# Identity products ahead of TensorE's first work, and the last layer's weights folded between the first transposes

## The chip, the cores and the metric

The kernel runs on one core of a Trainium2 chip. The metric is device microseconds of one execution of the whole program; lower is better. The kernel is compared by the median of three executions. Engines are named as in the profile: PE is TensorE's matmul side and PEld its weight loads, DVE is VectorE, ACT ScalarE, POOL GpSimd, and SP the queue that issues most of the transfers. TensorE runs at one of two clocks, 1.2 and 2.4 GHz; a granted clock of 0.5 in a view is the lower, 1.0 the higher.

## What is computed

Four graph layers with a residual around each are applied to `x` (8 batches, 1024 nodes, 256 features) with the same dense weighted adjacency `adj` (8 x 1024 x 1024, mostly zeros). All data are float32.

```
h = relu(layernorm(x)); q, k = split(h @ Wqk); v = h @ Wv          # layer 0
agg = adj @ k; w = sum(q * agg) / 16;  x = x + softmax(w)[:, None] * v
h = relu(layernorm(x)); x = x + attention(h, 8 heads, scores * 2 adj) @ Wo + bo   # layer 1
h = relu(layernorm(x)); x = x + hypergraph(h, W1, b1, gamma, beta, W2, b2) + h    # layer 2
h = relu(layernorm(x)); Q = h Wq^T + bq; K = h Wk^T + bk; V = h Wv^T + bv         # layer 3
w = adj * exp(Q K^T); x = x + (w / rowsum(w)) @ V
```

Several products of weights alone are made once, before the loop over the batches, and used in all of them. Layer 0: Wq0 Wk0^T, so that `w` is the row sum of (h Wq0 Wk0^T) times (adj h). Layer 3: M3 = Wq3^T Wk3 in the same way, the vectors Wq3^T bk3 and Wk3^T bq3, and the number bq3 . bk3. Layer 2: gamma W2 and beta W2; layer 1: bv1 Wo1, which joins the output's bias.

## The kernel before, in words

The five engines run programs of their own, written out by hand in `build_program`, and meet by semaphores; no scheduler moves anything. The order of instructions in the code is the order in which each engine takes them, and an engine whose next instruction waits holds all that stand behind it. Batch 0 is written out for TensorE (`batch(0, True)`), the others run in a loop. Nodes stand in eight tiles of 128 (NT = 8), features in two of 128 (DT = 2). PSUM is `ps` with eight banks of 512 columns. An fp32 product shows as two MATMUL records, a transpose as one.

What matters here is the setup and the first stage of batch 0, about the first 40 us:

- SP issues the transfers in this order: `xn` (the batch's x, 1 MB), `mask`, `wqk0s` and `W0`'s right half (layer 0's weights, signalled by `weights0_in`), then fourteen under `weights_in`: seven vectors (L423), `w2s`, `Wo1`, the two halves of `w3s` (Wq3 and Wk3), and three broadcasts `bo1B`, `b2B`, `bv3B`. Behind them come `adjT` (4 MB), three weights `W1`, and `adjN` (4 MB). At last SP waits for `m3_made` and stores M3s to `M3_kept`.
- POOL makes the constants `ident` and `ones` and three small things (`consts_ready` counts to 5), then layer norm's scales.
- ACT makes `h`, tiles 0 to 3 and then 4 to 7 (L976), copies the transposed `h` out of PSUM to `hT` (L984), and `G`, the projected tiles (L992).
- DVE makes layer norm's statistics, copies the first products to `W0` (L944, L945), multiplies h by the mask (`mh`, L666, eight tiles), spreads the vectors out (L951 to L954) after `weights_in`, and copies the folded products out: `cs`, `bo1B`, `cB` after `setup_pe` 2, `fold` after 3, `M3s` after 4 (L957 to L963).
- PE waits for `weights0_in`, multiplies wqk0s into banks 0 and 1, transposes h tiles 0 to 3 (`transpose_h(b, 0, 0)`, L1166), waits for all of `mhs` (the eight `mh` tiles), transposes tiles 4 to 7, waits for `hTs`, runs `project_g` (16 products with W0), then `fold_weights` (L1126, through the helper `product`), and after all of its results have been copied out (`setup_dve` 7 and `m3_made`), `aggregates(0)` to `aggregates(7)`: adj h, 64 products. These read `adjT`.

Of the kernel before, what the change touches and what calls it, by code (L numbers as in the profile page):

```python
# [7 lines left out]
ALU = mybir.AluOpType  # L8
# [3 lines left out]
P = 128  # L12
# [19 lines left out]
def build_program(nc, x_in, adj_in, adjT_in, mask_in, wqkT0, wv0, w1attn, bq1, bk1, bv1, bo1,  # L32
                  w1T, b1, gamma, beta, w2T, b2, w3attn, bq3, bk3, bv3, out):
    B, N, D = x_in.shape
    NT = N // P
    DT = D // P
# [3 lines left out]
    FT = HID // P  # L40
# [23 lines left out]
    with ctx:  # L64
        def sb(name, shape, dt=F32, scope=ctx):
            return scope.enter_context(nc.sbuf_tensor(name, shape, dt))

        def signal(name, per):
            return Signal(ctx.enter_context(nc.semaphore(name)), per)
# [3 lines left out]
        ident = sb("ident", [P, P])  # L73
        ones = sb("ones", [P, P])
        W0 = sb("W0", [P, DT, 2 * D])
        Wo1 = sb("Wo1", [P, DT, D])
        bq1c = sb("bq1c", [P, DT])
        bk1c = sb("bk1c", [P, DT])
        bq3c = sb("bq3c", [P, DT])
        bk3c = sb("bk3c", [P, DT])  # L80
        gammac = sb("gammac", [P, FT])
        betac = sb("betac", [P, FT])
        cs = sb("cs", [P, D])
        bo1B = sb("bo1B", [P, D])
# [3 lines left out]
        cB = sb("cB", [P, D])  # L88
# [22 lines left out]
        def region(*layouts):  # L111
            got = []
            for i, layout in enumerate(layouts):
                with ExitStack() as scope:
                    got.append([sb(n if i == 0 else f"{n}_{i}", s, d, scope) for n, s, d in layout])
            sizes = [sum(_bytes(s) for _, s, _ in layout) for layout in layouts]
            sb(f"region_{layouts[0][0][0]}", [P, max(sizes) // 4])
            return got
# [27 lines left out]
        h, hT, mh, G = a0  # L146
        qS, kS = a1
        _, HT, Uh, Ul, A2T = a2
        _, t3T, _, v3, _, W3v, M3, hT3 = a3

        _, M3s, wqk0s, betaB, w3s, w2s, bqk, gammaB, bvB, bv1c = asetup
# [15 lines left out]
        _, PTb, rs, Rs = p1b  # L167
# [4 lines left out]
        _, shiftB, b1B = p2c  # L172
# [8 lines left out]
        ps = ctx.enter_context(nc.psum_tensor("ps", [P, 8, HALF], F32))  # L181
# [8 lines left out]

        weights0_in = signal("weights0_in", 0)
        weights_in = signal("weights_in", 0)
        consts_ready = signal("consts_ready", 0)
        beta_bc = signal("beta_bc", 0)
        setup_pe = signal("setup_pe", 0)
        setup_dve = signal("setup_dve", 0)
# [16 lines left out]
        m3_made = signal("m3_made", 0)  # L213
# [88 lines left out]
        rd3 = signal("rd3", NT)  # L302
        x3s = signal("x3s", NT)

        NW = 7 + 3 + 4

        def stand(engine, waited):

# [73 lines left out]
        def agg_bank(t):  # L382
            return t if t < 2 else 6 + t % 2
# [13 lines left out]
        def rows(t):  # L397
            return slice(t * P, (t + 1) * P)
# [22 lines left out]
        def _(sp):  # L421
            def load(dst, src):
                sp.dma_start(dst, src).then_inc(weights_in.sem, 16)  # L423
# [17 lines left out]
            load_x(0)  # L441
            sp.dma_start(wqk0s[:], wqkT0.rearrange("(t p) d -> p t d", p=P)).then_inc(weights0_in.sem, 16)
            sp.dma_start(W0[:, :, D:2 * D], wv0.rearrange("(t p) d -> p t d", p=P)).then_inc(weights0_in.sem, 16)
            for dst, src in ((gammac, gamma), (betac, beta), (bv1c, bv1), (bq3c, bq3), (bk3c, bk3), (bq1c, bq1),
                             (bk1c, bk1)):
                load(dst[:], src)
            load(w2s[:], w2T.rearrange("(t p) d -> p t d", p=P))
            load(Wo1[:], w1attn[3].rearrange("(t p) d -> p t d", p=P))
            for i in range(2):
                load(w3s[:, i], w3attn[i].rearrange("(t p) d -> p t d", p=P))  # L450
            for dst, src in ((bo1B, bo1), (b2B, b2), (bv3B, bv3)):
                load(dst[:], src.partition_broadcast(P))
            load_adjT(0)
# [170 lines left out]
        def _(dve):  # L624
# [36 lines left out]
            def scale_mask():  # L661
                dve.tensor_scalar(mask16[:], mask[:], W_SCALE, None, ALU.mult).then_inc(chain.sem, 1)
# [285 lines left out]
            scale_mask()  # L948
            dve.wait_ge(weights_in.sem, 16 * NW)
            for t in range(FT):  # L950
                dve.tensor_copy(betaB[:, t], betac[:, t:t + 1].broadcast_to([P, P])).then_inc(beta_bc.sem, 1)  # L951
                dve.tensor_copy(gammaB[:, t], gammac[:, t:t + 1].broadcast_to([P, P])).then_inc(beta_bc.sem, 1)
            for c in range(DT):
                dve.tensor_copy(bvB[:, c], bv1c[:, c:c + 1].broadcast_to([P, P])).then_inc(beta_bc.sem, 1)  # L954
            dve.tensor_tensor(bqk[:], bq3c[:], bk3c[:], ALU.mult).then_inc(setup_dve.sem, 1)
            dve.wait_ge(setup_pe.sem, 2)
            dve.tensor_copy(cs[:], ps[:, 0, 0:D]).then_inc(setup_dve.sem, 1)  # L957
            dve.tensor_tensor(bo1B[:], ps[:, 1, 0:D], bo1B[:], ALU.add).then_inc(setup_dve.sem, 1)
            dve.tensor_copy(cB[:], ps[:, 2, 0:D]).then_inc(setup_dve.sem, 1)
            dve.wait_ge(setup_pe.sem, 3)  # L960
            dve.tensor_copy(fold[:], ps[:, 3, 0:2 * DT + 1]).then_inc(setup_dve.sem, 1)
            dve.wait_ge(setup_pe.sem, 4)
            dve.tensor_copy(M3s[:].rearrange("p c d -> p (c d)"), ps[:, 6]).then_inc(m3_made.sem, 1)  # L963
            with dve.Fori(0, B - 1) as b:
                batch(b, False)
            batch(B - 1, True)
# [155 lines left out]
        def _(pe):  # L1122
            def product(dst, pairs):

                for i, (lhsT, rhs) in enumerate(pairs):
                    mm = pe.matmul(dst, lhsT, rhs, start=(i == 0), stop=(i == len(pairs) - 1))  # L1126
                return mm

            pe.wait_ge(weights0_in.sem, 32)
            for a in range(DT):  # L1130
                mm = product(ps[:, a, 0:D], [(wqk0s[:, c, rows(a)], wqk0s[:, DT + c]) for c in range(DT)])
            mm.then_inc(setup_pe.sem, 1)
            pe.wait_ge(consts_ready.sem, 5)

            def fold_weights():
                pe.wait_ge(setup_dve.sem, 2)
                pe.wait_ge(weights_in.sem, 16 * NW)
                pe.wait_ge(beta_bc.sem, 2 * FT + DT)
                product(ps[:, 0, 0:D], [(gammaB[:, t], w2s[:, t]) for t in range(FT)])
                product(ps[:, 1, 0:D], [(bvB[:, c], Wo1[:, c]) for c in range(DT)])  # L1140
                product(ps[:, 2, 0:D], [(betaB[:, t], w2s[:, t]) for t in range(FT)]).then_inc(setup_pe.sem, 1)
                for a in range(DT):
                    product(ps[:, 3, a:a + 1], [(w3s[:, 0, c, rows(a)], bk3c[:, c:c + 1]) for c in range(DT)])
                for a in range(DT):
                    product(ps[:, 3, DT + a:DT + a + 1], [(w3s[:, 1, c, rows(a)], bq3c[:, c:c + 1]) for c in range(DT)])
                pe.wait_ge(setup_dve.sem, 3)
                product(ps[:, 3, 2 * DT:2 * DT + 1], [(ones[:], bqk[:, c:c + 1]) for c in range(DT)]).then_inc(setup_pe.sem, 1)
                for c in range(DT):
                    mm = product(ps[:, 6, D * c:D * (c + 1)], [(w3s[:, 1, o, rows(c)], w3s[:, 0, o]) for o in range(DT)])
                mm.then_inc(setup_pe.sem, 1)  # L1150
                pe.wait_ge(setup_dve.sem, 7)
                pe.wait_ge(m3_made.sem, 1)

            def keep_warm(bank, count):

# [4 lines left out]
            def transpose_h(b, k, s):  # L1160

                for c in range(DT):
                    for a in range(TPH):
                        t = TPH * s + a
                        pe.wait_ge(*hs(b, NT * k + t + 1))
                        mm = pe.transpose(ps[:, 4 + 2 * s + c, rows(a)], h[:, t, rows(c)], ident[:])  # L1166
                    mm.then_inc(hT_ps.sem, 1)

            def batch(b, first):

                def aggregates(t):
                    if t >= 4:
                        pe.wait_ge(*wrs(b, t - 1))
                    product(ps[:, agg_bank(t), 0:D], [(adjT[:, j, rows(t)], mh[:, j]) for j in range(NT)]).then_inc(agg_ps.sem, 1)

                transpose_h(b, 0, 0)

                pe.wait_ge(*mhs(b, NT))
                transpose_h(b, 0, 1)
                def project_g():  # L1180
                    pe.wait_ge(*hTs(b, 2 * DT))
                    for t in range(NT):
                        if t >= 2:
                            pe.wait_ge(*gs(b, t - 1))
                        product(ps[:, 4 + t % 2, 0:D], [(hT[:, c, rows(t)], W0[:, c, 0:D]) for c in range(DT)]).then_inc(g_ps.sem, 1)

                if first:
                    pe.wait_ge(setup_dve.sem, 2)
                    project_g()
                    fold_weights()  # L1190
                pe.wait_ge(*adjT_in_s(b, 16))
                aggregates(0)
                if not first:
                    project_g()
                for t in range(1, NT):
                    aggregates(t)
                def values(t):
# [334 lines left out]
                for t in range(NT):  # L1532
# [4 lines left out]
                    product(ps[:, 6 + t % 2, 0:D + 1], [(P3[:, s, j, rows(a)], v3[:, j, 0:D + 1]) for j in range(NT)]).then_inc(o3_ps.sem, 1)  # L1537

            batch(0, True)
            with pe.Fori(1, B) as b:  # L1540
                batch(b, False)
# [43 lines left out]
```

## Time and profile before

| | |
|---|---|
| median of three executions | 2977.01 us |
| lowest to highest | 2976.28 to 2977.42 us |
| profiled execution, its own time | 2976.45 us |
| its span, first to last instruction | 2974.6 us |
| PE busy | 2929.9 us, 98% of the span |
| DVE, ACT, POOL busy | 63%, 50%, 24% |
| mean granted clock of TensorE | 0.998 |

The profiled execution has its own time beside its span: 1.85 us lie around the span. A busy PE here is one that has a record running; the time of a record depends on the granted clock. In the page's 40 slices (74 us each) PE stands at 9 in all but the first, where it is at 8.

### The profile page before, as it was taken

What the parts mean: (1) busy time and instruction counts of PE and PEld (TensorE: products, weight loads), DVE (VectorE), ACT (ScalarE), POOL (GpSimd) and SP (SyncE); (2) the same over time, 40 slices, a digit from 0 to 9 for tenths busy, and PEclk for the clock granted to TensorE, in tenths of its full rate; (3) what the DMA queues carried; (4) which work ended last, traced back from release to release, by engine and by line L of the source; (5) the groups of instructions that cost most, each with busy time, mean ns of one, the idle gap of its engine ahead of it and who ended that gap; (6) DMA issues with size and microseconds to landing.
All of it is one profiled execution on the core that took longest, in us unless ns stands there. A gap on an engine that the chain in (4) does not pass through costs nothing.

```text
span 2974.6 us, 63498 instructions
## 1 busy us (share of the span) xinstructions
PE 2929.9 (98%) x23040; PEld 2376.7 (80%) x23040; DVE 1869.7 (63%) x4154; ACT 1476.8 (50%) x2761; POOL 719.9 (24%) x1305
## 2 busy tenths in 40 slices
PE   8999999999999999999999999999999999999999
PEld 6787787887878878788788886888868888688886
DVE  3797427974278742887428874388643886438862
ACT  1783317833178332883328732387323873238722
POOL 0343003420034201342013420134201341014410
PEclk9999999999999999999999999999999999999999
DMA  5202212022120231201311113111222021220200
GB/s 175 93 2 93 81 69 93 2 93 100 54 90 7 88 119 42 83 31 64 135 39 70 57 48 125 58 51 63 61 107 78 32 77 69 84 78 30 83 8 15
DMA packets 95317, 204.29 MB, mean 69 GB/s; under 512 B 10512, under 2 KB 41616, under 8 KB 94992
## 3 DMA queue, kind: packets, MB, share of 16 engines
q1 hardware_dynamic: 93456, 195.76, 18.0%
q8 instruction: 203, 3.33, 0.5%
q0 software_dynamic: 1536, 4.20, 0.4%
q14 instruction: 122, 1.00, 0.1%
HBM read 136.75 MB, written 8.65 MB: 49 GB/s over the span
## 4 chain that ended last, share of the span: by engine, by line
PE 82%; DVE 12%; ACT 3%; issue 2%; DMA 0%; DVEq 0%; ACTq 0%; SPq 0%
PE ps L1126 39%; PE ps L1314 15%; PE ps L1343 8%; PE ps L1292 8%; PE ps L1407 7%; PE ps L1482 4%; DVE junk L836 3%; DVE stats L633 1%; DVE h L852 1%; DVE dn L845 1%; DVE h L870 1%; PE ps L1166 1%; DVE shiftB L867 1%; ACT Uh L1093 1%; DVE Ul L678 1%
## 5 line engine op out<-in xcount | busy, mean ns | idle before, releaser
L794 DVE CUSTOM_DVE_ANT_0 Z<-ps,adjN 128x1024 f32<-128x1024 f32 x512 | 622.5, 1217 | 44.5 <-PE ps L1292 36.9
L1050 ACT ACTIVATE Z<-Z,nm 128x1024 f32<-128x1024 f32 x512 | 590.2, 1153 | 5.2 <-POOL nm L570 5.2
L1314 PE MATMUL ps<-ident,Z 128*128 128x128 f32 x4096 | 539.0, 275 | 2.2 <-ACT Z L1050 1.2
L1314 PEld LDWEIGHTS ps<-ident,Z 128*128 128x128 f32 x4096 | 463.7, 140 | 91.2 <-issue 42.5
L1292 PE MATMUL ps<-kS,qS 128*128 128x512 f32 x1024 | 372.8, 446 | 2.3 <-issue 1.8
L582 POOL TENSOR_SCALAR H<-adjN 128x128 fp32r<-128x128 f32 (+1 forms) x456 | 317.5, 696 | 0.0
L570 POOL TENSOR_TENSOR nm<-nm,minus 128x1 f32<-128x1 f32 x512 | 97.1, 190 | 557.0 <-DVE nm L794 556.6
L1126 PE MATMUL ps<-mh,adjT 128*128 128x256 f32 x1024 | 223.6, 379 | 0.8 <-issue 0.8
L1126 PE MATMUL ps<-v,P 128*128 128x257 f32 x1024 | 223.6, 379 | 0.0
L1126 PE MATMUL ps<-hT,t3T 128*128 128x512 f32 x512 | 221.0, 592 | 0.0
L1126 PEld LDWEIGHTS ps<-v,P 128*128 128x128 f32 x1024 | 193.9, 189 | 31.8 <-issue 3.8
L1126 PEld LDWEIGHTS ps<-mh,adjT 128*128 128x128 f32 x1024 | 194.1, 190 | 27.1 <-issue 1.2
L1343 PE MATMUL ps<-PTb,v 128*32 128x128 f32 x3456 | 201.9, 274 | 0.8
L1343 PE MATMUL ps<-PTa,v 128*32 128x128 f32 x3456 | 201.9, 274 | 0.0
L1126 PEld LDWEIGHTS ps<-hT,t3T 128*128 128x128 f32 x512 | 97.3, 190 | 119.0 <-issue 118.6
L1126 PE MATMUL ps<-W,hT 128*128 128x256 f32 x768 | 180.7, 386 | 11.1 <-DVE qlo L734 8.2
L1343 PEld LDWEIGHTS ps<-PTb,v 128*32 128x32 f32 x3456 | 174.0, 110 | 20.3 <-issue 17.6
L1343 PEld LDWEIGHTS ps<-PTa,v 128*32 128x32 f32 x3456 | 174.0, 110 | 17.7 <-issue 17.7
L547 POOL TENSOR_SCALAR ve<-mv 128x4 f32<-128x4 f32 x64 | 12.7, 198 | 724.4 <-DVE mv L638 723.7
L690 DVE CUSTOM_DVE_ANT_0 E<-ps,G 128x256 f32<-128x256 f32 x64 | 27.2, 424 | 252.4 <-PE ps L1126 209.4
L1040 ACT ACTIVATE PTa<-ps 128x512 f32<-128x512 f32 x240 | 140.2, 595 | 77.4 <-PE ps L1314 77.4
L1040 ACT ACTIVATE PTb<-ps 128x512 f32<-128x512 f32 x248 | 144.3, 597 | 66.2 <-PE ps L1314 66.2
(183 smaller groups left out, 5894.9 us busy)
## 6 DMA issues: line engine op xcount, KB each, us to landing
adjT<-adjT_in SPq DMA_DIRECT2D x8, 4096.0 KB, 13.2
adjN<-adj_in SPq DMA_DIRECT2D x8, 4096.0 KB, 17.2
adjT<-adjT_in SPq DMA_DIRECT2D x8, 2048.0 KB, 11.8
qS<-qhi SPq DMA_DIRECT2D x112, 128.0 KB, 2.1
qS<-qlo SPq DMA_DIRECT2D x112, 128.0 KB, 2.1
adjT<-adjT_in SPq DMA_DIRECT2D x8, 1536.0 KB, 6.4
xn<-x_in SPq DMA_DIRECT2D x8, 1024.0 KB, 5.8
out<-x SPq DMA_DIRECT2D x8, 1024.0 KB, 4.9
```

The source lines that it names most:

```text
L570: pool.tensor_tensor(nm[:, u:u + 1], nm[:, u:u + 1], minus[:], ALU.mult).then_inc(nms.sem, 1)
L582: done = pool.tensor_scalar(H[:, t, of], adjN[:, t, of], 0.0, 0.0, ALU.is_equal, ALU.is_equal)
L794: dve.tensor_tensor_reduce(Z[:, u % ZS], ps[:, 2 * (u % 2):2 * (u % 2) + 2].rearrange("p a n -> p (a n)"), adjN[:, u // HEADS], SCORE_SCAL ...
L836: dve.scalar_tensor_tensor(junk[:], H[:, t].bitcast(F32), 1.0, wB[:], ALU.mult, ALU.mult, accum_out=dn[:, 0, t:t + 1]).then_inc(dns.sem, 1)
L1040: act.activation(PT(u)[:, first:first + NT // 2], heads_of(ps[:, bank]), ACT.Copy).then_inc(PT_act.sem, 1)
L1050: act.activation(Z[:, u % ZS], Z[:, u % ZS], ACT.Exp, bias=nm[:, u:u + 1], accum_out=sm[:, u:u + 1]).then_inc(exps.sem, 1)
L1126: mm = pe.matmul(dst, lhsT, rhs, start=(i == 0), stop=(i == len(pairs) - 1))
L1292: mm = pe.matmul(ps[:, 2 * (u % 2) + s], qS[:, hd, rows(t)], kS[:, hd, half(s)], start=True, stop=True)
L1314: mm = pe.transpose(ps[:, turn_bank((u, s)), rows(a)], Z[:, u % ZS, rows(NT // 2 * s + a)], ident[:])
L1343: mm = pe.matmul(ps[HD * j:HD * j + HD, 7, P * (g % GROUPS):P * (g % GROUPS + 1)], v[:, kt, HD * hd:HD * hd + HD], PT(HPG * g + j)[:, kt], ...
L1407: mm = pe.matmul(dst(n, i), lhs(n, j, i), rhs(n, j, i), start=(j == 0 and i == 0), stop=(j == NT - 1 and i == 0))
L1482: mm = pe.matmul(ps[:, bank(t), 0:D], HT[:, j, rows(t)], (Vh, Vl)[i][:, j], start=(j == 0 and i == 0), stop=(j == NT - 1 and i == 0))
```

## The change

Three things are done.

PE waits for the constants and makes 16 products of `ident` with `ones` (128 x 128 each, into bank 7, which nobody reads) before it waits for `weights0_in`.

The two halves of `w3s` and the vectors bq3, bk3 are issued by SP right behind `W0`'s right half, ahead of the other vectors, and have a signal of their own, `w3s_in`. `weights_in` counts ten transfers in place of fourteen. The bytes in all are the same.

`fold_weights` is split. The part on w3s is `fold_scores`: M3 (into bank 2 in place of 6) and the two vectors (bank 3) are made right after the transposes of tiles 0 to 3. The rest (gamma W2, bv1 Wo1, beta W2, bq3 . bk3) stays behind `project_g`, in banks 0, 0 (right half), 1 and 3. DVE copies M3s first, then cs, bo1B, cB and fold. PE waits for `setup_dve` 5 (cs and bo1B, both of bank 0) before `aggregates(0)`, and for 7 and `m3_made` before `aggregates(1)`.

```diff
-        NW = 7 + 3 + 4
+        NW = 5 + 2 + 3
+        WARM = 16
...
-            for dst, src in ((gammac, gamma), (betac, beta), (bv1c, bv1), (bq3c, bq3), (bk3c, bk3), (bq1c, bq1),
-                             (bk1c, bk1)):
+            for i in range(2):
+                sp.dma_start(w3s[:, i], w3attn[i].rearrange("(t p) d -> p t d", p=P)).then_inc(w3s_in.sem, 16)
+            for dst, src in ((bq3c, bq3), (bk3c, bk3)):
+                sp.dma_start(dst[:], src).then_inc(w3s_in.sem, 16)
+            for dst, src in ((gammac, gamma), (betac, beta), (bv1c, bv1), (bq1c, bq1), (bk1c, bk1)):
                 load(dst[:], src)
...
-            for i in range(2):
-                load(w3s[:, i], w3attn[i].rearrange("(t p) d -> p t d", p=P))
...
+            dve.wait_ge(w3s_in.sem, 16 * 4)
             dve.tensor_tensor(bqk[:], bq3c[:], bk3c[:], ALU.mult).then_inc(setup_dve.sem, 1)
             dve.wait_ge(setup_pe.sem, 2)
+            dve.tensor_copy(M3s[:].rearrange("p c d -> p (c d)"), ps[:, 2]).then_inc(m3_made.sem, 1)
+            dve.wait_ge(setup_pe.sem, 3)
             dve.tensor_copy(cs[:], ps[:, 0, 0:D]).then_inc(setup_dve.sem, 1)
-            dve.tensor_tensor(bo1B[:], ps[:, 1, 0:D], bo1B[:], ALU.add).then_inc(setup_dve.sem, 1)
-            dve.tensor_copy(cB[:], ps[:, 2, 0:D]).then_inc(setup_dve.sem, 1)
-            dve.wait_ge(setup_pe.sem, 3)
+            dve.tensor_tensor(bo1B[:], ps[:, 0, D:2 * D], bo1B[:], ALU.add).then_inc(setup_dve.sem, 1)
+            dve.tensor_copy(cB[:], ps[:, 1, 0:D]).then_inc(setup_dve.sem, 1)
+            dve.wait_ge(setup_pe.sem, 4)
             dve.tensor_copy(fold[:], ps[:, 3, 0:2 * DT + 1]).then_inc(setup_dve.sem, 1)
-            dve.wait_ge(setup_pe.sem, 4)
-            dve.tensor_copy(M3s[:].rearrange("p c d -> p (c d)"), ps[:, 6]).then_inc(m3_made.sem, 1)
...
+            pe.wait_ge(consts_ready.sem, 5)
+            for _ in range(WARM):
+                pe.matmul(ps[:, NT - 1, 0:P], ident[:], ones[:], start=True, stop=True)
             pe.wait_ge(weights0_in.sem, 32)
...
+            def fold_scores():
+                pe.wait_ge(w3s_in.sem, 16 * 4)
+                for c in range(DT):
+                    mm = product(ps[:, 2, D * c:D * (c + 1)], [(w3s[:, 1, o, rows(c)], w3s[:, 0, o]) for o in range(DT)])
+                mm.then_inc(setup_pe.sem, 1)
...
                 transpose_h(b, 0, 0)
+                if first:
+                    fold_scores()
 
                 pe.wait_ge(*mhs(b, NT))
                 transpose_h(b, 0, 1)
...
                 pe.wait_ge(*adjT_in_s(b, 16))
+                if first:
+                    pe.wait_ge(setup_dve.sem, 5)
                 aggregates(0)
```

On PE, from its first matmul to the start of the aggregates, before (`ps<-ident,h` are the transposes, `ps<-W,hT` is `project_g`, `ps<-mh,adjT` the aggregates):

```order
L1126 MATMUL ps<-wqk0s 128x256 x4
L1166 MATMUL ps<-ident,h 128x128 x16
L1126 MATMUL ps<-W,hT 128x256 x16
L1126 MATMUL ps<-w2s,gammaB 128x256 x4
L1126 MATMUL ps<-Wo,bvB 128x256 x2
L1126 MATMUL ps<-w2s,betaB 128x256 x4
L1126 MATMUL ps<-bk3c,w3s 128x1 x4
L1126 MATMUL ps<-bq3c,w3s 128x1 x4
L1126 MATMUL ps<-bqk,ones 128x1 x2
L1126 MATMUL ps<-w3s 128x256 x4
L1126 MATMUL ps<-mh,adjT 128x256 x64
```

The same stretch of PE in the changed kernel, up to the aggregates, which come next:

```order
L1135 MATMUL ps<-ones,ident 128x128 x16
L1130 MATMUL ps<-wqk0s 128x256 x4
L1172 MATMUL ps<-ident,h 128x128 x8
L1130 MATMUL ps<-w3s 128x256 x4
L1130 MATMUL ps<-bk3c,w3s 128x1 x4
L1130 MATMUL ps<-bq3c,w3s 128x1 x4
L1172 MATMUL ps<-ident,h 128x128 x8
L1130 MATMUL ps<-W,hT 128x256 x16
L1130 MATMUL ps<-w2s,gammaB 128x256 x4
L1130 MATMUL ps<-Wo,bvB 128x256 x2
L1130 MATMUL ps<-w2s,betaB 128x256 x4
L1130 MATMUL ps<-bqk,ones 128x1 x2
```

Sixteen identity products are new at the head; four products and eight one-column products on w3s moved from behind `project_g` to between the two halves of the transposes.

On SP, the transfers behind those of layer 0's weights in the changed kernel (before, `bq3c` and `bk3c` stood in fourth and fifth place behind `gammac`, `betac`, `bv1c`, and the two of `w3s` behind `Wo`):

```order
L445 DMA W<-wv 128x2x256
L447 DMA w3s<-wq 128x2x256
L447 DMA w3s<-wk 128x2x256
L449 DMA bq3c<-bq 128x2
L449 DMA bk3c<-bk 128x2
L425 DMA gammac<-gamma 128x4
L425 DMA betac<-beta 128x4
L425 DMA bv1c<-bv 128x2
L425 DMA bq1c<-bq 128x2
L425 DMA bk1c<-bk 128x2
```

Four transfers moved ahead of seven; what is ahead of `adjT` is the same set.

## Rows read from the trace of the kernel before

**Rows 1.** The page: the span and the engines' busy time.

```profile
span 2974.6 us, 63498 instructions
PE 2929.9 (98%) x23040; PEld 2376.7 (80%) x23040; DVE 1869.7 (63%) x4154; ACT 1476.8 (50%) x2761; POOL 719.9 (24%) x1305
```

**Rows 2.** Chain that ended last, first 40 us: start, duration (us), what.

```profile
2.41 6.48 DMA W<-wv
...
8.94 3.78 PE ps L1126 x8
12.71 0.02 issue
12.73 0.42 DVE W L944
13.16 0.33 DVE W L945
13.49 2.11 DVE mh L666 x8
...
15.64 1.73 PE ps L1166 x8
17.37 0.02 issue
17.40 0.61 ACT hT L984
18.00 0.14 issue
18.14 17.72 PE ps L1126 x80
35.85 0.83 issue
36.69 3.48 PE ps L1126 x15
```

**Rows 3.** Timeline of PE, 0 to 40 us: start, duration, group, [idle before].

```profile
8.94 3.76 PE L1126 MATMUL ps<-wqk0s 128*128 128x256 f32 x8 [8.94 <-DMA W<-wv]
12.51 1.06 PE L1166 MATMUL ps<-ident,h 128*128 128x128 f32 x8
15.64 1.71 PE L1166 MATMUL ps<-ident,h 128*128 128x128 f32 x8 [2.08 <-DVE mh L666]
18.14 9.44 PE L1126 MATMUL ps<-W,hT 128*128 128x256 f32 x32 [0.78 <-ACT hT L984]
27.41 1.89 PE L1126 MATMUL ps<-w2s,gammaB 128*128 128x256 f32 x8
29.14 1.03 PE L1126 MATMUL ps<-Wo,bvB 128*128 128x256 f32 x4
30.00 1.89 PE L1126 MATMUL ps<-w2s,betaB 128*128 128x256 f32 x8
31.73 0.95 PE L1126 MATMUL ps<-bk3c,w3s 128*128 128x1 f32 x8
...
33.43 0.58 PE L1126 MATMUL ps<-bqk,ones 128*128 128x1 f32 x4
33.88 1.97 PE L1126 MATMUL ps<-w3s 128*128 128x256 f32 x8
36.69 3.69 PE L1126 MATMUL ps<-mh,adjT 128*128 128x256 f32 x16 [0.83 <-issue]
```

**Rows 4.** Busy time by stretch: engines busy (x instructions), PEclk granted, DMA share, GB/s.

```profile
8.94:12.51 3.57, 3.57 (x8) 2.75 (x9) 1.19 (x7) 2.08 (x5) 2.19 (x3) 1.00 1.09 311
...
15.64:17.37 1.73, 1.71 (x8) 1.31 (x8) 0.17 (x3) 0.60 (x1) 0.00 (x0) 0.59 0.93 357
18.14:22.54 4.40, 4.40 (x11) 3.51 (x12) 0.60 (x5) 0.95 (x2) 0.00 (x0) 0.50 1.03 415
22.54:27.41 4.87, 4.87 (x23) 4.10 (x22) 0.00 (x0) 2.37 (x5) 0.00 (x0) 0.97 1.04 392
```

**Rows 5.** Timelines of POOL, DVE and ACT around the setup, same columns.

```profile
1.63 0.09 POOL L539 MEMSET minus<- 128x1 f32 x1
...
12.30 0.16 DVE L645 SCALAR_TENSOR_TENSOR nmr<-mv,rstd 128x4 f32<-128x4 f32 x1 [1.52 <-POOL rstd L549]
...
32.27 0.41 DVE L958 TENSOR_TENSOR bo1B<-ps,bo1B 128x256 f32<-128x256 f32 x1
...
35.89 0.69 DVE L963 COPY M3s<-ps 128x512 f32<-128x512 f32 x1 [1.67 <-PE ps L1126]
...
10.16 2.07 ACT L976 ACTIVATE h<-xn,nmr,rstd 128x256 f32<-128x256 f32 x4 [8.12 <-DVE nmr L645]
...
14.48 1.05 ACT L984 ACTIVATE hT<-ps 128x512 f32<-128x512 f32 x2
```

**Rows 6.** Transfers of the first 60 us: KB each, us from issue to landing.

```profile
adjT<-adjT_in SPq DMA_DIRECT2D x1, 4096.0 KB, 17.5
...
w3s<-wk SPq DMA_DIRECT2D x1, 256.0 KB, 5.1
```

**Rows 7.** Timeline of SP: when transfers were issued.

```profile
8.04 0.47 SPq L423 DMA_DIRECT2D w3s<-wk  x1
...
10.01 0.43 SPq L437 DMA_DIRECT2D adjT<-adjT_in  x1
```

More of the change, by code:

```diff
@@ L192, in build_program @@
         weights_in = signal("weights_in", 0)
+        w3s_in = signal("w3s_in", 0)
         consts_ready = signal("consts_ready", 0)
@@ L1132, in _ @@
             mm.then_inc(setup_pe.sem, 1)
[L1133 to L1141, printed above, removed]
+            def fold_scores():
[3 more added lines that the diff above has]
+                mm.then_inc(setup_pe.sem, 1)
                 for a in range(DT):
@@ L1145, in fold_weights @@
                     product(ps[:, 3, DT + a:DT + a + 1], [(w3s[:, 1, c, rows(a)], bq3c[:, c:c + 1]) for c in range(DT)])
+            def fold_weights():
+                pe.wait_ge(weights_in.sem, 16 * NW)
+                pe.wait_ge(beta_bc.sem, 2 * FT + DT)
+                product(ps[:, 0, 0:D], [(gammaB[:, t], w2s[:, t]) for t in range(FT)])
+                product(ps[:, 0, D:2 * D], [(bvB[:, c], Wo1[:, c]) for c in range(DT)])
+                product(ps[:, 1, 0:D], [(betaB[:, t], w2s[:, t]) for t in range(FT)]).then_inc(setup_pe.sem, 1)
                 pe.wait_ge(setup_dve.sem, 3)
                 product(ps[:, 3, 2 * DT:2 * DT + 1], [(ones[:], bqk[:, c:c + 1]) for c in range(DT)]).then_inc(setup_pe.sem, 1)
[L1148 to L1152, printed above, removed]
             def keep_warm(bank, count):
@@ L1194, in batch @@
                     project_g()
+                else:
+                    pe.wait_ge(setup_dve.sem, 7)
+                    pe.wait_ge(m3_made.sem, 1)
                 for t in range(1, NT):
```

## The prediction

> **What bounds the kernel now.** I read the page first: the span is 2974.6 us and PE is busy for 98% of it [rows 1]. A kernel in that state gets shorter only where PE idles, where it runs at the lower clock, or where it does less work. The change touches only the setup and the first stage of batch 0, so the next view is the chain that ended last over the first 40 us [rows 2]. There the end of each step starts the next one: layer 0's weights land at 8.89, PE multiplies them, DVE copies the two results and makes the eight `mh` tiles, PE transposes tiles 4 to 7, ACT copies, PE runs 80 records (project_g and the folds) from 18.14 to 35.85, and after 0.83 us more the aggregates start at 36.69. From there on PE has its work in a fixed order and is busy. So the whole question is at which time the aggregates start; what that instant moves by, the end moves by, unless something with a clock of its own (a transfer) is late for it.
>
> The third view is PE's timeline [rows 3] with the granted clock by stretch [rows 4]. Two things are to be seen. First the pace. Records of 256 columns come 0.216 us apart at the full clock: the 20 from 27.41 to 31.73 took 4.32 us. The 32 of project_g took 9.27 us (18.14 to 27.41) where 32 x 0.216 = 6.91 would do, because the granted clock was 0.50 from 18.14 to 22.54. The transposes of tiles 4 to 7 had 0.59 and took 1.71 us, while those of tiles 0 to 3 took 1.06 us. The first eight records (wqk0s) took 3.76 us, 0.47 each, twice the pace of the same shape at 27.41; that is the lower clock, 1.2 GHz, although the view prints 1.00 there. I go by the pace: the view has no change of clock to show before the first rise. Second, the idle: PE stood 8.94 us at the start and 2.08 us (13.57 to 15.64) waiting for `mh`, and the clock was down behind that second gap.
>
> **The change, part by part.** The sum is made against the profiled execution, 2976.45 us (span 2974.6 and 1.85 around it); the median of the three is 2977.01, 0.56 above.
>
> *Identity products.* The constants are ready at 1.63 + 0.09 = 1.72 [rows 5]. 16 products are 32 records of 128 columns. At the lower clock a record of 128 columns costs half of 0.43, 0.21 us (1.71 us for eight transposes, mostly at that clock, [rows 3]), so they run from about 1.9 to 8.7 if the clock never rises, and end sooner if it does, at half that, 0.11 a record (near 7.2, if it rises after 18 of the 32). Both ends are ahead of 8.94, when layer 0's weights let PE start: cost nothing. They read two SBUF tiles and write bank 7, whose first user is the second half of the transposes. If they ran longer than I say by 1 us, the wqk0s products would start 0.8 us later and still be done before DVE can take them, if they run at the full clock.
>
> *The wqk0s products at the full clock.* Eight records take 1.9 us in place of 3.76 and end near 10.9. What is late next: DVE, which has its `nmr` at 12.30 to 12.46 ahead of the copies [rows 5]. So the copies start at 12.46 in place of 12.73 and `mh` is complete 0.27 us sooner, near 15.35. A gain of 0.27 at most on that branch.
>
> *fold_scores between the transposes.* The h tiles 0 to 3 end at 12.23 [rows 5], so the transposes of the first half are through near 12.83 (five of them still to come, 0.11 us apart). Then M3, eight records: 1.97 us busy at 33.88, less the 0.16 us by which a group overlaps its follower (1.89 against 29.14 - 27.41 = 1.73), so 1.81. Then 16 one-column records: 33.43 - 31.73 = 1.70. PE is free at 12.83 + 1.81 + 1.70 = 16.34, with small switches 16.4. The cover of this work is the gap up to 15.35, and about 1 us sticks out of it: the second transposes start at 16.4 in place of 15.64, 0.75 us later. Behind PE's new wait for `w3s_in` stand those transposes, then ACT's copies, then project_g. Its price: `w3s` was on chip at 8.04 + 5.1 = 13.1 with nine more transfers issued ahead of it than now [rows 6, 7]. At 13.1 it would cost 0.3 us; two of 256 KB right behind `W<-wv`, which lands at 8.89, should be there near 10.5 to 11. I take no wait, and keep 0.3 for the range.
>
> *Second transposes and copies at the full clock.* Before, 15.64 to 18.14 took 2.50. At the full clock the eight transposes take 1.06 in place of 1.71; ACT starts its first copy after four of them (0.69), two copies in a row take 1.05 [rows 5], and 0.14 to PE [rows 2]: 1.9. project_g starts at 18.3, 0.15 us later than before.
>
> *project_g at the full clock.* 32 x 0.216 = 6.91 and a few hundredths for the first: it ends at 25.25 in place of 27.41. Here 2.3 us are won, by the clock alone.
>
> *What is left of the folds.* gamma, bv and beta take 1.73 + 0.86 + 1.89 = 4.48 to the last result. Then 0.04 to DVE, `cs` 0.34 ahead of `bo1B`, which takes 0.41 (32.27 to 32.68 for results of 31.89), and 0.11 from DVE to PE (36.58 to 36.69). Together 5.4: the aggregates start at 25.25 + 5.4 = 30.65. Before, from 27.41 it took 9.28. Won here: 3.9 us, the M3 and one-column products and M3's copy (0.69) and its waits. The four records of bqk lie beside DVE's copies. The wait for `setup_dve` 7 and M3 ahead of aggregates(1) is 3.5 us later and met; DVE's new wait for `w3s_in` is met since before 17.
>
> *What is late next.* `adjT` lands at 10.01 + 17.5 = 27.5 [rows 6, 7]. The same bytes stand ahead of it as before, so it has 3.1 us to spare. Later stages of the batch need nothing that comes at a fixed time.
>
> Sum: 36.69 - 30.65 = 6.0 us. That is 2970.4 from the profiled execution and 2971.0 from the median. I forecast **2970.8**. A measurement of this kernel can tell about 0.2%, 5.95 us, from no change: 2971.06 is the border, and the forecast lies on it.
>
> **The rivals.**
>
> *Rival 1, the clock falls again.* Where the clock does rise by the identity products before 8.94, they can end near 7.2, and 1.7 us of idle follow; and from 10.9 to 12.3 PE only has transposes as h comes. In the trace the clock was down after a gap of 2.08 us. If it falls in one of these gaps and is up again by 12.5, the first products take 3.76 as before and fold_scores starts 0.7 later: 2971.5. If it falls once later, so that the second transposes and project_g run as in rows 4, 0.6 + 2.3 = 2.9 us come back: 2973.7. By the one-column products the array also has little to do for 1.70 us, which speaks for it; against it, the clock did not fall around the 20 of them at 31.73 to 33.88. The Trainium skill (TensorE: Matmul & The Clock Gate, section "HAM oscillation — how this bites in real kernels") says that waits for a transfer between short bursts of products take the clock back down each time; by that rule the identity products lose part of what they bring and this rival holds. The trace agrees so far as its one gap goes.
>
> *Rival 2, slower than before.* The clock goes down at the one-column products, in front of the transposes, and stays down through project_g, the folds and the first aggregate. Each 256-column record then costs 0.21 more: 0.6 + 32 x 0.21 + 20 x 0.21 + 16 x 0.21 = 14.9 us, 2985.3. It decides from 6.0 us lost (no gain), some 28 records, and for slower by 0.2% from 12 us, some 55 records at the lower clock on the path. Against it: the lower clock ended after 4.4 us of unbroken work, 11 records [rows 4], and all of this stretch is unbroken.
>
> *Rival 3, the transfer takes over.* If the new order made `adjT` land later than 30.65, the aggregates would wait for it; at 34 the time is 2973.8. Nothing in the rows says so, as nothing is added ahead of it.
>
> **How the numbers follow.** Forecast, full clock on the path from 12.5 on: 0.60, within 2970.2 to 2971.6, and three quarters of that under the border. Rival 1: 0.30, 2971.5 to 2973.7, most of it short of 0.2%. Rival 2: 0.03. Rival 3: 0.04, within 0.2%. 0.03 for a larger gain, where executions before paid more for the lower clock than the profiled one (the three reach 2977.42). So faster by over 0.2%: 0.48; within 0.2%: 0.48; slower: 0.04. The range takes in the forecast, both values of rival 1 with the 0.56 us between the profiled execution and the median, and the sum less 0.6: 2969.8 to 2974.3.
>
> **What would show it.** Right: the wqk0s records 0.22 us apart; M3's records begin near 12.8 and the second transposes near 16.4; project_g takes under 7.1 us from about 18.3; the aggregates start near 30.7. Wrong: a granted clock of 0.5 anywhere between 12.5 and 30, a wait for w3s before M3, a wait for adjT ahead of the aggregates, or aggregates that start at 30.7 with an end that moved by less.

## The result: slower by 0.39%, with the first stage as forecast

The changed kernel takes 2987.71 us (median of six, 2983.83 to 2988.56) against 2976.30 us before (six, 2972.51 to 2977.42): the ratio is 1.0039, interval 1.0028 to 1.0049. The forecast was 2970.8 us with a range up to 2974.3. It is wrong in its sign and by 17 us.

The profiled execution has 2987.93 us and a span of 2986.1. Its page begins so; the line of PE answers to the one in [rows 1]:

```profile
span 2986.1 us, 63562 instructions
PE 2936.6 (98%) x23072; PEld 2382.9 (80%) x23072; DVE 1868.7 (63%) x4154; ACT 1477.4 (49%) x2761; POOL 719.9 (24%) x1305
...
q8 instruction: 203, 3.33, 0.5%
```

32 records more on PE and 32 on PEld, and 64 instructions more in all (63562 against 63498 in [rows 1]): these are the 16 identity products. The page calls queue q8 "instruction"; its 203 packets of 3.33 MB are 16 KB each.

PE's timeline over the first 40 us, to be laid beside [rows 3]:

```profile
1.78 5.71 PE L1135 MATMUL ps<-ones,ident 128*128 128x128 f32 x32 [1.78 <-POOL minus L542]
8.61 1.99 PE L1130 MATMUL ps<-wqk0s 128*128 128x256 f32 x8 [1.11 <-DMA W<-wv]
...
12.93 1.89 PE L1130 MATMUL ps<-w3s 128*128 128x256 f32 x8
...
16.36 1.07 PE L1172 MATMUL ps<-ident,h 128*128 128x128 f32 x8
18.26 7.14 PE L1130 MATMUL ps<-W,hT 128*128 128x256 f32 x32 [0.83 <-ACT hT L988]
25.24 1.89 PE L1130 MATMUL ps<-w2s,gammaB 128*128 128x256 f32 x8
...
30.66 19.66 PE L1130 MATMUL ps<-mh,adjT 128*128 128x256 f32 x90 [0.60 <-DVE bo1B L964]
```

The aggregates of batch 0 start at 30.66, where 30.65 was forecast; 6.03 us are won there. The span is 11.5 us longer all the same, so 17.5 us are lost behind that point (2986.1 - 2974.6 + 6.0).

Where they are lost, the starts of the aggregates show. In the kernel before, these stand at 397.90 in batch 1 and at 2603.98 in batch 7, 2206.1 us apart; in the changed one at 391.42 and 2614.09, 2222.7 apart. The six batches between hold 16.6 us of the loss. The other 0.9 are 1.4 lost behind 2614.09, where the clock fell once more, less 0.5 won between 30.66 and 391.42. What PE waited for in the six batches:

```profile
PE ps L1172 <- issue: 15.3, 6, 3.0
PE ps L1130 <- DVE qlo L737: 6.0, 6, 1.0
```

The columns are us in total, times, longest. "Issue" means that nothing which the profile shows held the engine: six times, once per batch, 15.3 us. The same view of the kernel before has no such line for the transposes. It has this one, at layer 1's scores:

```profile
PE ps L1292 <- issue: 1.8, 3, 0.8
```

The first of the six on PE's timeline of the changed kernel, and below it the same place in the kernel before:

```profile
755.84 0.41 PE L1172 MATMUL ps<-ident,h 128*128 128x128 f32 x2
758.67 1.75 PE L1172 MATMUL ps<-ident,h 128*128 128x128 f32 x14 [2.41 <-issue]
760.25 3.62 PE L1130 MATMUL ps<-mh,adjT 128*128 128x256 f32 x16
```

```profile
764.01 1.11 PE L1166 MATMUL ps<-ident,h 128*128 128x128 f32 x8
765.29 1.10 PE L1166 MATMUL ps<-ident,h 128*128 128x128 f32 x8 [0.17 <-DVE mh L666]
766.23 3.62 PE L1126 MATMUL ps<-mh,adjT 128*128 128x256 f32 x16
```

PE makes two transposes of a new batch and then runs nothing for 2.41 us, though nothing in the profile holds the third. It happens in batches 2 to 7, never in batch 1: batch 0 is written out and batch 1 is entered from above, while batches 2 to 7 are entered by a jump back. The jumps are in the trace as well, at the loop's line (duration in ns, shortest, median and longest; first and last start in us):

```profile
L1553 PEldq COMPARE_BRANCH  x7: 83/3596/3849, 752.0 to 2976.6; - x7
```

The one of 83 ns is the last, which is not taken; the six that are take 3.3 to 3.8 us each. Around the first of them, from 752.05 to 755.65, the transfers of the instruction queue (stretches 752 to 754 us and 756 to 757 us of the changed kernel; packets, MB, share):

```profile
q8 instruction: 1, 0.02, 3.7%
...
q8 instruction: 1, 0.02, 5.9%
```

One packet of 16 KB starts at 753.09, 1.0 us after the jump began, and the jump ends 2.6 us later. The next starts only at 756.41, and 2.3 us after that PE goes on. While the jump lasts PE does not idle: records that it already held run on until the first transpose at 755.84.

In some batches the clock then falls too. In the changed kernel (stretch; its length; busy us and instructions of PE, PEld, DVE, ACT and POOL; granted clock; share and GB/s of the transfers):

```profile
1125.74:1127.91 2.17, 0.00 (x1) 0.00 (x0) 0.74 (x3) 0.00 (x0) 0.00 (x0) 1.00 0.28 97
1128.73:1132.14 3.41, 3.41 (x14) 3.05 (x13) 0.00 (x0) 1.93 (x4) 0.00 (x0) 0.50 0.52 172
1132.14:1140.00 7.86, 7.86 (x37) 6.67 (x37) 0.43 (x2) 2.37 (x5) 0.00 (x0) 1.00 0.00 0
```

The lower clock lies over the rest of the transposes and the first aggregates. PE's timeline there:

```profile
1127.91 2.51 PE L1172 MATMUL ps<-ident,h 128*128 128x128 f32 x14 [2.27 <-issue]
1130.21 4.58 PE L1130 MATMUL ps<-mh,adjT 128*128 128x256 f32 x16
```

In batch 2 the same groups took 1.75 and 3.62 us, so the clock cost 1.7 us here, on top of the 2.27. It was at 0.5 in batches 3, 5, 6 and 7, once each, and each fall came 0.8 to 1.4 us after the end of the idle time.

### The profile page after: what moved, and what is told of

It is laid out like the page before. It is cut to its first block, busy times and chain, and to the rows that moved or that the text cites. A ratio compares the mean times of both kernels' runs of the same rounds, so it can differ in the third digit from the quotient of the medians.

```text
span 2986.1 us, 63562 instructions
## 1 busy us (share of the span) xinstructions
PE 2936.6 (98%) x23072; PEld 2382.9 (80%) x23072; DVE 1868.7 (63%) x4154; ACT 1477.4 (49%) x2761; POOL 719.9 (24%) x1305
## 3 DMA queue, kind: packets, MB, share of 16 engines
q8 instruction: 203, 3.33, 0.5%
## 4 chain that ended last, share of the span: by engine, by line
PE 82%; DVE 11%; ACT 4%; issue 3%; DVEq 0%; DMA 0%; ACTq 0%; POOL 0%; SPq 0%; POOLq 0%
PE ps L1130 39%; PE ps L1327 14%; PE ps L1356 8%; PE ps L1305 7%; PE ps L1420 7%; PE ps L1495 4%; DVE junk L839 3%; DVE stats L636 1%; DVE h L855 1%; PE ps L1172 1%; DVE dn L848 1%; DVE h L873 1%; DVE shiftB L870 1%; ACT Uh L1097 1%; ACT Z L1054 1%
## 6 DMA issues: line engine op xcount, KB each, us to landing
adjN<-adj_in SPq DMA_DIRECT2D x8, 4096.0 KB, 17.5
```

## The experiments

Three theories were tried.

- A: the place of PE's code. The 64 instructions ahead of the loop move the jump's target to just ahead of a border between two of the blocks in which instructions arrive. PE runs what is left of the first block and waits for the second.
- B: the new order of the folds (banks, M3's early store, signals) holds PE.
- C: what matters is only where the clock's falls lie.

Some versions are padded with waits on a count that was reached at 1.7 us. Two such waits make one instruction: with 512 of them the page counts 256 instructions more (63754 against 63498). Times are medians (of one run each for the two with 256 and 320 instructions), with the kernel before run on the same chip.

### The changed kernel, 16 instructions further

```diff
+            for _ in range(32):
+                pe.wait_ge(consts_ready.sem, 5)
             pe.wait_ge(weights0_in.sem, 32)
```

> The changed kernel with 16 more PE instructions ahead of its loop over the batches (32 more waits on a count that has been reached, in the time in which PE waits for layer 0's weights); no work is added or taken away. Theory A, place of the code: PE's jump back lands just ahead of a border of the blocks in which its instructions are brought, and 16 instructions carry the target over that border. Then the six idle times of 2.3 to 3.0 us behind the first two transposes of batches 2 to 7 are gone, no clock falls there, the aggregates of batch 0 still start near 30.7, and the time is 2976.3 - 6 = 2970 (2967 to 2972). Theory B, something in the new order of the folds (banks, M3's early store, signals) holds PE in each batch: the idle times stay, 2987.5. Theory C, the length of the loop's batches depends on where the clock's falls lie in time: the idle times stay at about 2.4 us, the time between 2983 and 2988.

Measured: 2968.25 us (2967.03 to 2969.34), before 2975.73; ratio 0.9974 (0.9965 to 0.9983). The answer on waits has no line of "issue" for the transposes. Batch 2 at its start, from PE's timeline:

```profile
758.18 1.03 PE L1174 MATMUL ps<-ident,h 128*128 128x128 f32 x8
759.46 1.10 PE L1174 MATMUL ps<-ident,h 128*128 128x128 f32 x8 [0.24 <-DVE mh L669]
760.40 3.62 PE L1130 MATMUL ps<-mh,adjT 128*128 128x256 f32 x16
```

Against the kernel before, each time, the changed kernel loses 11.4 us and this one wins 7.5: sixteen instructions that do nothing are worth 18.9 us. B and C fall.

The page of this version has one more thing to show:

```profile
q8 instruction: 197, 3.23, 0.5%
```

Six packets fewer than the 203 of the changed kernel, for six jumps: with the target carried over the border, each pass of the loop that follows a jump takes one block less.

One number was missed: the aggregates of batch 0 start at 32.38, since the clock fell in the first stage here (project_g took 8.69 us, granted 0.50 from 18.2 to 21.5):

```profile
18.44 8.69 PE L1130 MATMUL ps<-W,hT 128*128 128x256 f32 x32 [0.83 <-ACT hT L988]
```

```profile
18.20:21.50 3.30, 3.06 (x7) 2.53 (x8) 1.35 (x8) 0.57 (x2) 0.00 (x0) 0.50 1.02 415
```

That is the prediction's rival 1, in a smaller size.

### The kernel before, 64 instructions further

The same two lines with 128 waits, in the kernel before; no product, no new order.

> The kernel before with 64 more PE instructions ahead of its loop (128 more waits on a count that has been reached, while PE waits for layer 0's weights): as many as the changed kernel has more than the kernel before, with none of its products and none of its new order. Theory A: the jump's target lies where it lies in the changed kernel, so six idle times of 2.3 to 3.0 us behind the first two transposes of batches 2 to 7 appear, and the time is 2976.3 + 15 to 17 = 2991 to 2994. Theories B and C: no idle times, 2976 to 2977.

Measured: 2993.39 us (2990.14 to 2994.92); ratio 1.0062 (1.0047 to 1.0078). Waits, and the start of batch 2:

```profile
PE ps L1168 <- issue: 15.9, 6, 2.9
```

```profile
761.38 0.38 PE L1168 MATMUL ps<-ident,h 128*128 128x128 f32 x2
764.03 2.33 PE L1168 MATMUL ps<-ident,h 128*128 128x128 f32 x14 [2.26 <-issue]
```

This is the loss of the changed kernel, made from the kernel before by waits alone, and the idle time stands behind the same second transpose.

### The identity products alone, and the folds alone

The first is the kernel before with the `WARM = 16` loop of the diff; the second the changed kernel with `WARM = 0`, which by the page has one instruction more than the kernel before (63499).

> The kernel before with the 16 identity products alone, 64 PE instructions. Theory A: the idle times of the changed kernel in full, and of the gain only what the clock brings in the first stage: the wqk0s products 1.7 us shorter (hidden up to 0.3), the clock as it falls or not at the gap ahead of the second transposes (0 to 2.9); 2988 to 2994. Theory B: no idle times, 2973.5 to 2976.5.

Measured: 2991.12 us (2988.18 to 2992.15), ratio 1.0054 (1.0039 to 1.0069). "Issue" held the transposes six times, 14.5 us. The first products take 1.99 us in place of 3.76, and the clock falls again in the gap ahead of the second transposes, as before:

```profile
8.96 1.99 PE L1126 MATMUL ps<-wqk0s 128*128 128x256 f32 x8 [1.97 <-DMA W<-wv]
...
15.31 1.97 PE L1169 MATMUL ps<-ident,h 128*128 128x128 f32 x8 [2.23 <-DVE mh L666]
18.06 8.96 PE L1126 MATMUL ps<-W,hT 128*128 128x256 f32 x32 [0.78 <-ACT hT L984]
...
36.13 9.09 PE L1126 MATMUL ps<-mh,adjT 128*128 128x256 f32 x41 [0.83 <-issue]
```

The aggregates start at 36.13 where they started at 36.69. What the identity products bring by themselves, these profiles do not settle: the padded version above, which has none, starts its aggregates at 35.50, because the clock was low for a shorter time there. By the medians this version is 2.3 us below the padded one, and their ranges overlap.

> The changed kernel without its identity products: the folds split and moved, w3s early, as many PE instructions as the kernel before has. Theory A: no idle times in the loop; the first products at the lower clock, the aggregates of batch 0 near 31.4 to 33, 2971 to 2974. Theory B: idle times as in the changed kernel, 2988 to 2990.

Measured: 2971.45 us (2970.02 to 2972.93), ratio 0.9988 (0.9979 to 0.9997). There is no idle time behind the jumps. The folds now lie between the two halves of the transposes, the clock stays up from 12.84 on to the last 3 us, and the aggregates start at 31.14, somewhat ahead of the 31.4 to 33 expected. In this profile all but 0.5 us of the first stage's gain is there without the identity products:

```profile
8.68 3.75 PE L1130 MATMUL ps<-wqk0s 128*128 128x256 f32 x8 [8.68 <-DMA W<-wv]
...
18.73 7.14 PE L1130 MATMUL ps<-W,hT 128*128 128x256 f32 x32 [0.83 <-ACT hT L988]
...
31.14 14.05 PE L1130 MATMUL ps<-mh,adjT 128*128 128x256 f32 x64 [0.60 <-DVE bo1B L964]
```

### The border moved by 16 and by 32 instructions the other way

`WARM = 12` and `WARM = 8` in the changed kernel.

> The changed kernel with 12 identity products in place of 16, so 16 PE instructions fewer ahead of the loop. Theory A with its numbers: the border of the block now lies 16 instructions further behind the jump's target, 8 transposes. The idle time stands behind about the tenth record of a batch in place of the second, and is shorter by the 8 x 0.11 us that PE now has in hand: about 1.5 us, six times, 9 us in all in place of 15.3; the time is 2970 + 9 to 11 = 2979 to 2981. A rival, that any jump onto a new block costs the same wherever in it the target lies: 2.4 us each at the same place, 2987.

Measured: 2980.87 us (2975.84 to 2983.11), ratio 1.0016 (1.0006 to 1.0026); "issue" 9.4 us, six times. Batch 2:

```profile
758.10 1.03 PE L1172 MATMUL ps<-ident,h 128*128 128x128 f32 x8
759.37 0.32 PE L1172 MATMUL ps<-ident,h 128*128 128x128 f32 x1 [0.24 <-DVE mh L669]
761.31 0.98 PE L1172 MATMUL ps<-ident,h 128*128 128x128 f32 x7 [1.61 <-issue]
```

The idle time stands behind the ninth record, about the tenth that was expected, and its total is near that of the sum (9). The rival with a fixed price falls.

> The changed kernel with 8 identity products, 32 PE instructions fewer ahead of the loop. Theory A: the border lies 32 instructions further on, behind the sixteen transposes; PE has 14 x 0.11 + 2 x 0.22 = 2.0 us more in hand, so 0.4 us or nothing is left of each idle time, 0 to 3 us in all; 2970 to 2974. The rival: 2987.

Measured: 2974.79 us (2973.17 to 2976.23), ratio 0.9997 (0.9987 to 1.0006). "Issue" is 4.7 us, six times, more than the 0 to 3 expected, and the time is 0.8 us above the 2970 to 2974:

```profile
756.70 2.20 PE L1172 MATMUL ps<-ident,h 128*128 128x128 f32 x15
759.51 0.27 PE L1172 MATMUL ps<-ident,h 128*128 128x128 f32 x1 [0.61 <-issue]
```

The idle time stands behind the fifteenth record of the batch, where 2 + 16 = 18 would be due at two instructions a record. The border moved by 13 records for 32 instructions, and PE had less in hand. Direction and order (2.5, 1.6 and 0.8 us each for 16, 12 and 8 products) are as expected; the exact count of instructions per record at this place I did not settle.

### 256 and 320 instructions

These are 512 and 640 waits in the kernel before, run once each.

> The kernel before with 256 more PE instructions ahead of its loop (512 more waits on a count that has been reached). Theory A, if blocks are 256 instructions: the target lies where it lies in the kernel before, so no idle time of over 1 us behind the first transposes, although more was added than in the kernel with 64. The waits may take longer than PE's idle start; then the first product is some us late. 2976 to 2984. A rival, that more code ahead of the loop is what costs: idle times of 2.4 us or more in batches 2 to 7, 2991 or more.

Measured: 2996.53 us, above the 2976 to 2984 expected. The term that was off is the price of the waits: PE's first product starts at 29.60, so 256 of them took 27.9 us, 0.109 us each, and I had no row for that. The aggregates of batch 0 start 20.6 us late (57.3), and with that taken off, the rest has the length of the kernel before: 2996.53 - 20.6 = 2975.9. On the theory the result is clear. There are four times as many instructions more as in the second experiment, and no idle time behind the second transpose:

```profile
784.43 1.04 PE L1168 MATMUL ps<-ident,h 128*128 128x128 f32 x8
785.71 1.10 PE L1168 MATMUL ps<-ident,h 128*128 128x128 f32 x8 [0.24 <-DVE mh L666]
```

> The kernel before with 320 = 256 + 64 more PE instructions ahead of its loop. Theory A: the idle times of 2.3 to 3.0 us are there again, behind the second transpose of batches 2 to 7, and the time is that of the kernel with 256 more plus 14 to 17 us.

Measured: 3019.74 us. With 64 instructions more than the last the idle time is back: "issue" held the transposes six times, 15.7 us.

```profile
787.88 0.49 PE L1168 MATMUL ps<-ident,h 128*128 128x128 f32 x2
790.95 2.31 PE L1168 MATMUL ps<-ident,h 128*128 128x128 f32 x14 [2.58 <-issue]
```

The difference to the last is 23.2 us, where 14 to 17 were expected without a price for the waits. 64 x 0.109 = 7.0 of it are waits, and the 16.2 left fit the range only by luck: the clock stayed up in the first stage here, so the aggregates of batch 0 start just 4.2 us later than in the last (61.45 against 57.27), and the loop lost 19.0 us, 15.7 in idle time and the rest where the clock fell behind it, four times.

Place counts, and not the amount of code. With 0 and with 256 instructions more there is no such idle time, with 64 and with 320 there is. That a block holds 256 and not half of that, the pages show: q8 moved 203 packets with 0 and with 64 instructions more, and with 256 and with 320 it moved one more.

```profile
q8 instruction: 204, 3.34, 0.5%
```

### Versions that keep the change and leave the border

The first is the changed kernel with `WARM = 20`. The second has `WARM = 17` and three identity products more, into bank 1, ahead of project_g; by the page it has 15 instructions more than the changed kernel (63577).

> The changed kernel with 20 identity products, 16 PE instructions more ahead of the loop. Theory A: as in the kernel with 16 instructions of waits, no idle times: 2968 (2966 to 2970). The four products more (0.9 to 1.7 us of PE's time) end ahead of layer 0's weights where the clock has risen by then, and hold the first products by up to 1.6 us where it has not, which DVE's chain hides.

Measured: 2966.71 us (2965.66 to 2968.23), before 2975.33; ratio 0.9973 (0.9962 to 0.9983). The clock rose once, at 6.8 us, and stayed up to the last 3 us; the aggregates start at 30.74 in batch 0, 391.51 in batch 1 and 2595.38 in batch 7, 2203.9 us for the six batches. That is 2.2 less than in the kernel before, whose own "issue" waits of 1.8 us at the scores are absent here. Those waits go by the target's place too: they are there, three times and 1.5 to 1.9 us in all, in the three kernels whose target lies where it lay before (0, 1 and 256 instructions more), once (0.5 us) in the one with 8 products, and in no other. Why they come so far behind the jump was not looked into. So part of the 8.6 us won against the kernel before is place and not the change: 5.95 by the start of the aggregates are the first stage.

> The changed kernel with 17 identity products at the head and 3 more of 128 columns in the 0.83 us in which PE waits for ACT's copies ahead of project_g; 15 PE instructions more ahead of the loop in all. Theory A: no idle times in the loop. If the clock's fall near 18 us (it was at 0.5 from 18.15 to 21.56 in one profile) comes from that gap, it is gone in more executions, and the time is 0.5 to 1.5 us below the kernel with 20 at the head: 2966.5 to 2968. If it comes from the one-column products or the waits for h, no difference.

Measured: 2965.98 us (2965.33 to 2967.24), ratio 0.9969 (0.9958 to 0.9980), 0.5 us below the range expected. The 0.83 us gap is filled:

```profile
17.25 0.83 PE L1198 MATMUL ps<-ones,ident 128*128 128x128 f32 x6
18.15 7.17 PE L1130 MATMUL ps<-W,hT 128*128 128x256 f32 x32
```

In both profiles the clock is up from the first 8 us to the last 3 or less, and the ranges of the two versions overlap, so what these three products bring (0.7 us by the medians) is open. The two are faster than the kernel before by 8.6 and 9.4 us, and so, with the 11.4 that the changed kernel loses against it, than the changed one by 20 and 21.

## Why the prediction was wrong

Step by step:

- *Identity products cost nothing* in the first stage: right, they ended at 7.5. In the program as a whole: wrong. They are the 64 instructions that moved the jump's target, and the text priced only their time.
- *First products at the full clock*: 1.99 us for 1.9, right; hidden behind DVE, as said.
- *fold_scores between the transposes*: M3 at 12.93 (12.83 forecast), second transposes at 16.36 (16.4). No wait for w3s. Right.
- *project_g at the full clock*: 18.26 to 25.24 for 18.3 to 25.25. Right in this execution; in the profiles of two of the experiments with the new order the clock fell here and project_g took 1.5 and 1.7 us longer.
- *The rest of the folds*: 5.42 us for 5.4. Right. The new wait on `bo1B` shows as 0.60 us.
- *"What that instant moves by, the end moves by, unless something with a clock of its own (a transfer) is late for it"*, and in *What is late next*, "Later stages of the batch need nothing that comes at a fixed time": this is the step that failed. I looked at data transfers and not at those that bring instructions, which do not move with the work but depend on where the jump's target lies in its block. The idle time that came of it is 15.3 us, and with the clock's falls behind it 17.5 us were lost where the text had nothing. The row on it was on the page of before (q8 instruction, 203 packets), and the loop's jump back was in the code.
- *Rivals*: rival 2 had the right sign, by a mechanism that did not occur; the clock fell in four batches, but only behind the idle times. Rival 1 occurs in the first stage of some executions, not in this one: beside the two with a slow project_g, the versions with 12 and with 8 products had the clock fall at 8.3 and 9.3 us, after PE had waited 2.5 and 3.2 us for layer 0's weights, and the first products took 3.48 and 3.26 us. Rival 3 did not occur: the aggregates waited for `bo1B`. The chances of the parts add up to 0.49 within 0.2% and 0.03 slower, where the text has 0.48 and 0.04; this changes nothing in the forecast.
- *The size of the first stage's gain*: 6.0 us forecast, 6.03 measured. The forecast's time was missed behind that point alone. A version with the change and another place of the target (16 instructions of waits) is 7.5 us faster than the kernel before, though its clock fell in the first stage and took back 1.7. Some of the 7.5 is the better place.

The Trainium skill has the rule (Runtime: NRT & Kernel Launch, section "Instruction fetch mechanics"): instructions come in 16 KiB blocks of 256, the next one is brought while the present one runs, and a taken branch to a block that is not held waits for it. The runs agree in the size of the packets (3.33 MB in 203) and the period (256 instructions: no idle; 320: idle). They also show the wait at the jump: the 72 taken jumps of the twelve profiles last 3.3 to 3.9 us each, and each ends 2.3 to 2.9 us after the start of a q8 packet. That wait was covered here: PE had records to run for the 3.8 us from 752.05, when the jump began, to the first transpose. What was not covered is the second block. Its packet starts 0.6 to 1.3 us after the end of every jump, with or without idle time, and PE runs out only where the target lies near the end of its block. In the four kernels with the target where it lies in the changed one PE goes on 2.2 to 2.9 us after that packet's start, much as each jump ends 2.3 to 2.9 us after the start of its own.

What is shown: that the idle time belongs to the number of instructions ahead of the loop modulo 256, that it shrinks as the border moves away from the target, and that the packets of q8 follow PE's code (edits of PE's program alone took their number from 203 to 197 or 204, and two follow each jump). What is argued from times alone: which block a given packet holds, and that the clock's falls in batches 2 to 7 follow from the idle time. For the latter speaks that the 24 idle times of 2.1 to 3.0 us in four kernels were followed by 13 falls, the six of 1.2 to 1.9 us by two, the six of 0.5 to 1.4 us by none, and that the other six profiles, which have no idle time behind the jump, have no fall there.

## What to carry to other kernels

An edit ahead of a loop is also an edit of where the loop's code lies. For an engine that is busy to the end and jumps back, count the instructions that the edit adds ahead of the target, look in the trace for "issue" idle time in the first records behind each jump, and compare the packets of the instruction queue between the two pages. If the idle time is there, enough instructions more to carry the target over the border (15 or 16 here) are a cheaper repair than any reordering; 16 or 32 fewer only made it shorter. An edit that was thrown out for a loss of some tenths of a per cent may deserve another try with another padding.

## What the runs showed of the hardware

- A taken jump back in PE's program lasted 3.3 to 3.9 us (72 of them in twelve profiles), one that is not taken 0.08 us. None of it showed as idle time of PE here, since PE had records to run meanwhile.
- Behind the jump PE idles by the place of its target: 2.1 to 3.0 us a jump where it lies in the changed kernel (four kernels), none with the target 15 or 16 instructions further on (three kernels), 1.2 to 1.9 with 16 instructions fewer ahead of it, 0.5 to 1.4 with 32 fewer. With the target where it lies in the kernel before (three kernels) it does not idle at the transposes, and 1.5 to 1.9 us in all at the scores.
- Instructions come in packets of 16 KB in a queue of their own. The six passes behind a jump took one packet less each when the target had crossed a border (197 in place of 203), and 256 instructions more ahead of the loop took one more (204).
- A wait of PE on a count already reached takes 0.109 us as an instruction that holds two such waits (27.9 us for 256).
- An idle time of 2.27 us was followed by 1.7 us more, as the clock was then granted at 0.5 from 1128.73 to 1132.14. It fell so in four of six batches of the changed kernel.
- Records of one column take 0.11 us each, yet the clock stayed up behind 16 of them in five of the seven profiles with the new order, and fell at 18.2 and 18.5 us in two (those with 16 instructions of waits and with 12 products).
